# A Mamba and mixture-of-experts block on one core: B and C projected as rows, read by ScalarE in slot 21

## The chip, the cores and the metric

The kernel runs on one core of one Trainium2 chip. The metric is the device time of one execution in microseconds (us); the figure for the kernel before is a median of three runs.

## What is computed

The input x has 32 sequences of 256 tokens with 128 channels. Three residual steps follow one another: half a mixture-of-experts FFN on the layernorm of x, a Mamba step on the layernorm of the result, and half the same FFN again. All is fp32.

```python
x = x + 0.5 * ffn(layernorm(x))
x = x + mamba(layernorm(x))
x = x + 0.5 * ffn(layernorm(x))
# in mamba(x):
x_in, z = split(x @ W_in + b_in)
x_conv = silu(causal_conv4(x_in))
Bm, Cm = split(x_conv @ W_xp + b_xp)          # 16 states each
delta = softplus(x_conv @ W_dt + b_dt)
h_t = exp(delta_t * A) * h_(t-1) + delta_t * x_conv_t * Bm_t
y = sum_states(h * Cm) + D_skip * x_conv
out = layernorm(x + (y * silu(z)) @ W_out + b_out, alpha, beta)
```

The FFN (`ffn`) has a router that takes the best two of 8 experts of width 176 and a shared expert of width 352; the kernel computes all experts and weights them.

## The kernel before

The 32 sequences are cut into 16 groups of two, 512 tokens each. `iterations` runs k from -2 to 17; iteration k scans group k, while the group ahead is prepared (layernorm, convolution, projections), a later one runs through the first FFN and the one behind through the second. Every iteration has 32 slots, two for each of the 16 states. What an engine does in a slot stands in tables written out by hand: `PLAN` names the steps, `UNIT` says in which slot a chunk of 128 FFN rows begins, `SP_PLAN` orders SyncE's DMAs. `PLANS` and the like hold variants for the first and the last iterations; iterations 2 to 13 use `PLAN` itself. Each engine runs its queue in order, and semaphores tie them together.

One FFN chunk that begins in slot s goes like this. TensorE makes h1 and h2 in slot s (L1173, L1197) into two alternating PSUM buffers each. ScalarE takes silu of h1 in the same slot (L796). VectorE multiplies h2 in slot s+1 (L991) by a row of router weights, `wrow`, that SyncE has brought by DMA (L507), or by silu for the shared expert. GpSimd multiplies that by silu in slot s+2 (`gated`, L649). TensorE makes the down product into `ps_y` in slot s+4 (L1189). An h1 product waits for the silu two chunks before it, and an h2 product for VectorE's product two chunks before it.

One state of the scan goes like this, in even slots. TensorE spreads one row of B over all partitions (`row_b`, L1152) into the upper half of `ps_db`, VectorE multiplies it by `du` (L966) in the odd slot before, ScalarE has made the decays (L779), VectorE scans (`hist`, L1011), and GpSimd multiplies by the row of C (`prod`, L718), which came by DMA (`crow`). After every second product GpSimd issues a DMA that adds the pair into `yacc` (L735).

B is wanted as three bf16 parts that add up to the fp32 value, stacked on 96 partitions (`bT`), so that `row_b` is a bf16 product. The kernel before makes them so: step `xproj` (L1261) multiplies each of four token tiles by the 32 columns of `w_xp`, which gives tokens on partitions; `bparts` (L1074, L1075) on VectorE adds the bias and rounds; `bsplit` (L686 to L688) on GpSimd makes the other two parts; `cT` and `bT` turn C and B by four transposes each (L1131), and ScalarE copies them out of PSUM (L845, L848). SyncE stores C to a DRAM tensor and reads rows back, spread over partitions.

All small products share one PSUM buffer, `ps_m`. Their steps take it in turns in the order of the plan: `claim` waits until the step before has been read (`misc_taken`).

SyncE loads the constants of the Mamba step in iteration -2, slot 8 (`other_constants`, L543), between the `wrow` DMAs of the first FFN. In slot 22 it stores the finished x of an old group, waits for that, and loads the next, after `addy1` in slot 21 has added the last down product into x (L998).

## Time and profile before

| | |
|---|---|
| median of 3 runs | 1823.36 us (1817.59 to 1824.13) |
| profiled execution, its own time | 1825.36 us |
| profiled execution, span from first to last instruction | 1823.6 us |
| mean granted TensorE clock | 0.973 |
| busy: TensorE, VectorE, ScalarE, GpSimd | 1653.7, 1484.8, 1270.4, 1444.2 us |
| moved by DMA | 302.97 MB |

A busy time is the sum of an engine's instructions in the one profiled execution. A time of idleness in brackets stands before the instruction that ended it, with what released it. Matmul ends are modelled, so neighbours overlap in the rows; start to start is the surer measure. An fp32 product shows as two records.

### The profile page before, as it was taken

How to read it: one execution, taken by the hardware profiler on the slowest of the kernel's cores; microseconds unless marked ns; L12 is line 12 of the kernel's file. 1: busy time of each engine (PE TensorE's matmuls, PEld its weight loads, DVE VectorE, ACT ScalarE, POOL GpSimd, SP SyncE). 2: the span in 40 equal slices, each digit the busy share in tenths (PEclk: the TensorE clock that was granted, in tenths of full speed). 3: DMA queues.
4: the chain of work that ended last, by engine and by line, in shares of the span. 5: the costliest groups of instructions: out<-in, count | busy, mean ns of one | idle time of the engine just before them, and what ended most of it. 6: DMA issues, size and time to landing. Idle time of an engine off the chain costs nothing.

```text
span 1823.6 us, 24045 instructions
## 1 busy us (share of the span) xinstructions
PE 1653.7 (91%) x7378; PEld 999.5 (55%) x7378; DVE 1484.8 (81%) x2244; ACT 1270.4 (70%) x2034; POOL 1444.2 (79%) x1362
## 2 busy tenths in 40 slices
PE   7877688999999999999999999999999999976689
PEld 4543445566565555656555555655555565543356
DVE  3276789889898988989898998979898898978852
ACT  3375678787868777786877777787777778675522
POOL 5255778888888888888888888889898888887853
PEclk9999799999999999999999999999999999998789
DMA  6136568687777868686777868777686868677632
GB/s 183 41 94 156 143 150 205 160 195 174 186 185 165 195 153 199 153 201 169 183 184 169 197 159 193 178 185 186 160 207 152 191 167 192 168 162 179 161 88 76
DMA packets 120999, 302.97 MB, mean 166 GB/s; under 512 B 19267, under 2 KB 40486, under 8 KB 106662
## 3 DMA queue, kind: packets, MB, share of 16 engines
q0 software_dynamic: 18144, 124.26, 34.1%
q1 hardware_dynamic: 100214, 175.36, 34.0%
q10 hardware_dynamic: 2512, 1.81, 0.3%
q8 instruction: 58, 0.95, 0.2%
q14 instruction: 71, 0.58, 0.1%
HBM read 167.67 MB, written 5.24 MB: 95 GB/s over the span
## 4 chain that ended last, share of the span: by engine, by line
POOL 46%; DMA 23%; issue 15%; PE 8%; DVE 5%; ACT 2%; SPq 0%; POOLq 0%; DVEq 0%; ACTq 0%
DMA yacc<-prod 21%; POOL prod L718 19%; POOL gated L649 14%; POOL yacc L714 3%; PE ps_y L1189 3%; DVE hist L1011 2%; POOL yacc L735 1%; PE ps_h1a L1173 1%; DVE ps_db L966 1%; PE ps_h2b L1197 1%; PE ps_h2a L1197 1%; POOL xres L705 1%; PE ps_h1b L1173 1%; POOL rstdx L630 1%; POOL prob L672 1%
## 5 line engine op out<-in xcount | busy, mean ns | idle before, releaser
L718 POOL TENSOR_TENSOR prod<-hist,crow 128x1024 f32<-128x1024 f32 x224 | 557.2, 2487 | 224.4 <-DVE hist L1011 192.9
L1189 PEld LDWEIGHTS ps_y<-down_w,gated 128*128 128x128 f32 (+1 forms) x3584 | 476.7, 196 | 278.0 <-issue 167.4
L1011 DVE TENSOR_TENSOR_SCAN hist<-decay,ps_db 128x1024 f32<-128x1024 f32 x256 | 583.3, 2279 | 3.8 <-ACT decay L779 1.1
L649 POOL TENSOR_TENSOR gated<-gated,silu 128x512 f32<-128x512 f32 x352 | 492.8, 1446 | 71.0 <-DVE gated L991 67.7
L1189 PE MATMUL ps_y<-down_w,gated 128*128 128x128 f32 (+1 forms) x3584 | 492.0, 282 | 54.2 <-POOL gated L649 51.2
L966 DVE TENSOR_TENSOR ps_db<-du,ps_db 128x1024 f32<-128x1024 f32 x256 | 313.2, 1223 | 135.2 <-PE ps_db L1152 133.4
L779 ACT ACTIVATE decay<-delta,a_neg 128x510 f32<-128x510 f32 x512 | 326.8, 709 | 1.5
L796 ACT ACTIVATE silu<-ps_h1a 128x512 f32<-128x512 f32 (+1 forms) x224 | 132.9, 593 | 189.0 <-PE ps_h1a L1173 186.2
L1173 PE MATMUL ps_h1b<-xnT,up_w 128*128 128x512 f32 x448 | 234.5, 605 | 8.1 <-ACT silu L796 8.1
L1173 PE MATMUL ps_h1a<-xnT,up_w 128*128 128x512 f32 (+1 forms) x448 | 238.4, 614 | 1.4 <-ACT xnT L802 1.0
L1197 PE MATMUL ps_h2b<-xnT,up_w 128*128 128x512 f32 x448 | 236.4, 610 | 0.6 <-DVE gated L991 0.5
L1197 PE MATMUL ps_h2a<-xnT,up_w 128*128 128x512 f32 (+1 forms) x448 | 233.1, 602 | 3.7 <-DVE gated L991 3.7
L796 ACT ACTIVATE silu<-ps_h1b 128x512 f32<-128x512 f32 x224 | 133.0, 594 | 77.5 <-PE ps_h1b L1173 70.5
L991 DVE TENSOR_TENSOR gated<-ps_h2b,wrow 128x512 f32<-128x512 f32 x192 | 130.7, 681 | 68.0 <-DMA wrow<-w_rows 36.1
L779 ACT ACT_TABLE_LOAD x126 | 161.7, 1283 | 2.2
L796 ACT ACT_TABLE_LOAD x113 | 145.0, 1283 | 2.0
L1152 PE MATMUL ps_db<-bT,sel_b 96*128 96x512 bf16 x256 | 101.7, 397 | 40.2 <-DVE hist L1011 39.8
L991 DVE TENSOR_TENSOR gated<-ps_h2a,wrow 128x512 f32<-128x512 f32 x160 | 107.9, 674 | 26.6 <-PE ps_h2a L1197 21.4
L1141 PE MATMUL ps_m<-xnT,w_conv 128*128 128x512 f32 (+3 forms) x256 | 119.2, 599 | 5.1 <-ACT xnT L802 5.1
L1173 PEld LDWEIGHTS ps_h1a<-xnT,up_w 128*128 128x128 f32 (+1 forms) x448 | 86.3, 195 | 57.9 <-issue 44.9
L1173 PEld LDWEIGHTS ps_h1b<-xnT,up_w 128*128 128x128 f32 x448 | 78.6, 192 | 66.3 <-issue 37.7
L735 POOL DMA_DIRECT2D yacc<-prod x111 | 100.8, 909 | 2.3 <-issue 2.3
(139 smaller groups left out, 1931.0 us busy)
## 6 DMA issues: line engine op xcount, KB each, us to landing
yacc<-prod POOLq DMA_DIRECT2D x111, 1024.0 KB, 9.9
crow<-c_rows SPq DMA_DIRECT2D x128, 512.0 KB, 5.0
wrow<-w_rows SPq DMA_DIRECT2D x320, 128.0 KB, 6.0
wrow<-w_rows SPq DMA_DIRECT2D x64, 224.0 KB, 7.3
wrow<-w_rows SPq DMA_DIRECT2D x64, 192.0 KB, 5.3
wrow<-w_rows SPq DMA_DIRECT2D x64, 160.0 KB, 3.0
yacc<-yacc POOLq DMA_DIRECT2D x15, 512.0 KB, 7.8
wrow<-w_rows SPq DMA_DIRECT2D x64, 96.0 KB, 3.0
```

The costliest lines, as they stand in the source:

```text
L649: nc.gpsimd.tensor_tensor(gated[:, pos % NGATE, :], gated[:, pos % NGATE, :], silu[:, (pos + NCHUNK * f_parity(of, f)) % NSILU, :], ALU.mu ...
L718: nc.gpsimd.tensor_tensor(prod[:, (pair - 1 + odd) % 2, s % 2, :, :], hist[:, s % 2, :, :], c_all, ALU.mult).then_inc(prod_done, 1)
L735: pool.dma_start(yacc[odd][:], prod[:, (pair - 1 + odd) % 2, :, :, :], accum_op=ALU.add).then_inc(acc_done, 16)
L779: ins = nc.scalar.activation(decay[:, s % NA, half, :, 1:LEN], d[:, :, 1:LEN], ACT.Exp, scale=a_neg[:, half, s:s + 1])
L796: nc.scalar.activation(silu[0:r, (pos + NCHUNK * f_parity(of, f)) % NSILU, :], ps_h1[pos % 2][0:r, :], ACT.Silu).then_inc(silu_done, 1)
L966: nc.vector.tensor_tensor(ps_db[:].rearrange("p (h t) -> p h t", h=HALVES), du[par][:], ps_db[:, TG:2 * TG].unsqueeze(1).to_broadcast([P, ...
L991: nc.vector.tensor_tensor(gated[0:r, pos % NGATE, :], ps_h2[pos % 2][0:r, :], factor, ALU.mult).then_inc(h2_taken, 1)
L1011: nc.vector.tensor_tensor_scan(hist[:, s % 2, :, :].rearrange("p h t -> p (h t)"), decay[:, s % NA, :, :, :].rearrange("p h b t -> p (h b ...
L1141: nc.tensor.matmul(acc[:, :, late:LEN], w_conv[:, tap, half * P:(half + 1) * P], now[:, :, 0:LEN - late], start=(tap == PAD), stop=False)
L1173: nc.tensor.matmul(ps_h1[pos % 2][0:r, :], up_w[:, 0, j * P:j * P + r], xnT[f][:], start=True, stop=True).then_inc(h1_full, 1)
L1189: ins = nc.tensor.matmul(ps_y[:, t * C:(t + 1) * C], gated[0:rd, posd % NGATE, t * P:(t + 1) * P], down_w[0:rd, jd, :], start=(posd == 0 a ...
L1197: nc.tensor.matmul(ps_h2[pos % 2][0:r, :], up_w[:, 1, j * P:j * P + r], xnT[f][:], start=True, stop=True).then_inc(h2_full, 1)
```

## The change

The projection gives rows at once. The weights `w_rows_bc` have 112 columns: the 16 of B at 0, 32 and 64, the 16 of C at 96, and zeros between. Two fp32 products of 512 tokens (one for each half of the 256 inputs) leave B three times and C once in `ps_m`, states on partitions. ScalarE reads the 96 rows of B with their bias, rounded to bf16, into `bT` (`b_high`), and then the 16 rows of C with their bias into `bounce`. VectorE takes bias + product - rounded value on the first 64 rows (`b_rest`), which frees `ps_m`. ScalarE rounds that into the first 64 rows of `bT` (`b_mid`), and GpSimd subtracts the middle part on the first 16 (`b_low`). So `bT` holds the low, the middle and the high part on its three blocks. `bparts`, `bsplit`, `cT` and `bT` are gone as steps; `bounce` has rows of its own for C. The constants come by eight DMAs in place of two, after VectorE has zeroed the padding.

```diff
@@ -56,8 +57,8 @@
         6: ["norm2", "rcopy0"], 7: ["gate_y0", "xT2"], 8: ["gate_y1", "in0a"], 9: ["in0"], 10: ["outproj"],
         11: ["resid", "route0"], 12: ["stats3", "in1a", "tilt0"], 13: ["in1", "scale3"], 14: ["in2", "ln_norm", "weights0"],
         15: ["in3", "ln_scale"], 16: ["wT0", "ln_shift"], 17: ["dt0"], 18: ["dt1", "ln_add"], 19: ["stats1"],
-        20: ["sp_exp", "xproj", "scale1"], 21: ["addy1"], 22: ["norm1", "sp_ln", "bparts"], 23: ["xT1", "bsplit"], 24: ["logits1"],
-        25: ["rcopy1", "route1"], 26: ["cT", "delta"], 27: ["bT", "tilt1"], 28: ["weights1", "du"], 30: ["wT1"],
+        20: ["sp_exp", "xproj", "scale1"], 21: ["addy1", "b_high"], 22: ["norm1", "sp_ln", "b_rest"], 23: ["xT1", "b_mid"], 24: ["logits1"],
+        25: ["rcopy1", "route1"], 26: ["delta"], 27: ["b_low", "tilt1"], 28: ["weights1", "du"], 30: ["wT1"],
     }
     EARLY = ("addy0", "addy1", "resid")
...
@@ -108,7 +109,7 @@
         24: ["store_w0@1", "w0:0@1", "w0:1@1", "w0:2@1", "w0:3@1"],
     }
     PLANS[-1] = {
-        0: ["sp_exp", "xproj"], 1: ["sp_ln", "bparts"], 2: ["bsplit", "a_neg"], 3: ["delta", "cT"], 4: ["bT"],
+        0: ["sp_exp", "xproj", "b_high"], 1: ["sp_ln", "b_rest"], 2: ["b_mid", "a_neg"], 3: ["delta"], 4: ["b_low"],
         5: ["du", "in2"], 6: ["in3"], 7: ["bias_parts"],
     }
     UNITS[-1] = {2: (0, 6), 4: (0, 7)}
@@ -116,8 +117,8 @@
     PLANS[0] = {
         1: ["stats0"], 2: ["scale0"], 3: ["norm0"], 6: ["xT0"], 7: ["logits0"], 8: ["rcopy0", "route0"], 9: ["addy0", "tilt0"],
         10: ["weights0", "stats2"], 11: ["scale2", "wT0"], 12: ["norm2"], 14: ["xT2"], 15: ["in0a"], 16: ["in0"],
-        17: ["in1a"], 18: ["in1"], 19: ["dt0"], 20: ["dt1"], 22: ["sp_exp", "xproj"], 23: ["sp_ln"], 24: ["bparts"],
-        25: ["bsplit", "in2"], 26: ["delta", "cT"], 27: ["bT"], 28: ["du", "in3"],
+        17: ["in1a"], 18: ["in1"], 19: ["dt0"], 20: ["dt1"], 22: ["sp_exp", "xproj", "b_high"], 23: ["sp_ln"], 24: ["b_rest"],
+        25: ["b_mid", "in2"], 26: ["delta"], 27: ["b_low"], 28: ["du", "in3"],
     }
     UNITS[0] = {pos - 8: (0, pos, -1) for pos in range(8, NCHUNK)}
...
@@ -367,12 +363,10 @@
         dtmp = sb("dtmp", [P, HALVES, TG])
         delta = [sb(f"delta{i}", [P, HALVES, TG]) for i in range(2)]
         du = [sb(f"du{i}", [P, HALVES, TG]) for i in range(2)]
-        bc = sb("bc", [P, TILES, 2 * NS])
-        brem = sb("brem", [P, TILES, NS])
-        bparts = sb("bparts", [P, TILES, KP], BF16)
+        brem = sb("brem", [64, TG])
         bT = [sb(f"bT{i}", [KP, TG], BF16) for i in range(2)]
-        bounce = sb("bounce", [NS, TG])
-        wT, cT = bounce[0:E, :], bounce
+        bounce = sb("bounce", [BC_ROWS, TG])
+        wT, cT = bounce[0:E, :], bounce[KP:BC_ROWS, :]
         NA, NC = 4, 4
         decay = sb("decay", [P, NA, HALVES, NSEQ, LEN])
...
@@ -477,7 +472,7 @@
             def rows_c(g, par, p):
 
                 if p == 0:
-                    sp.wait_ge(misc_taken, turn(g - 1, "cT"))
+                    sp.wait_ge(c_made, g + 1)
                     sp.dma_start(c_rows[par, :, :], cT[:]).then_inc(c_stored, 16)
                 if p > 1 or g > 0:
...
@@ -542,12 +537,20 @@
             def const(dst, src, sem):
                 sp.dma_start(dst, src).then_inc(sem, 16)
 
+            def dve_zeroed():
+
+                sp.wait_ge(pads_zero, 3)
+
             def other_constants():
                 with nc.allow_non_contiguous_dma(reason="small constants in column form"):
                     const(w_dt[:], W_dt.rearrange("(h p) n -> p h n", p=P), consts_loaded)
                     const(b_dt_c[:], b_dt.rearrange("(h p) -> p h", p=P), consts_loaded)
-                    const(w_xp[:], W_xp.rearrange("(h p) n -> p h n", p=P), consts_loaded)
-                    const(b_xp_b[:], b_xp.partition_broadcast(P), consts_loaded)
+                    dve_zeroed()
+                    for q in range(PARTS):
+                        const(w_rows_bc[:, :, 32 * q:32 * q + NS], W_xp[:, 0:NS].rearrange("(h p) n -> p h n", p=P), consts_loaded)
+                        const(b_rows_bc[32 * q:32 * q + NS, :], b_xp[0:NS].rearrange("(n o) -> n o", o=1), consts_loaded)
+                    const(w_rows_bc[:, :, KP:BC_ROWS], W_xp[:, NS:2 * NS].rearrange("(h p) n -> p h n", p=P), consts_loaded)
+                    const(b_rows_bc[KP:BC_ROWS, :], b_xp[NS:2 * NS].rearrange("(n o) -> n o", o=1), consts_loaded)
                     const(a_log[:], A_log.rearrange("(h p) s -> p h s", p=P), consts_loaded)
                     const(d_c[:], D_skip.rearrange("(h p) -> p h", p=P), consts_loaded)
...
@@ -679,14 +682,10 @@
                             nc.gpsimd.tensor_tensor(wtok[:], hotp[:, :, 0, :], hotp[:, :, 1, :], ALU.add
                                                     ).then_inc(wtok_ready, 1)
                             chain.end()
-                        elif step == "bsplit":
-                            pool.wait_ge(misc_taken, turn(it, "xproj"))
-                            chain = Chain(pool, pool_split, SPLIT_LINKS, it + 1)
-                            hi, md, lo = (bparts[:, :, 32 * q:32 * q + NS] for q in range(PARTS))
-                            chain.link(nc.gpsimd.tensor_tensor(md, bc[:, :, 0:NS], hi, ALU.subtract))
-                            chain.link(nc.gpsimd.tensor_tensor(brem[:], bc[:, :, 0:NS], hi, ALU.subtract))
-                            nc.gpsimd.tensor_tensor(lo, brem[:], md, ALU.subtract).then_inc(bparts_ready, 1)
-                            chain.end()
+                        elif step == "b_low":
+                            pool.wait_ge(b_mid_ready, it + 2)
+                            low = bT[nxt][0:NS, :]
+                            nc.gpsimd.tensor_tensor(low, brem[0:NS, :], low, ALU.subtract).then_inc(b_ready, 1)
                         elif step == "fold":
                             pool.wait_ge(acc_done, 16 * PAIRS * it)
...
@@ -836,17 +835,10 @@
                             take(it, step)
                             if route_no(it, step) > 0:
                                 act.wait_ge(w_stored, 16 * route_no(it, step))
-                            if bounced(it, step, ("cT",)) > 0:
-                                act.wait_ge(c_stored, 16 * bounced(it, step, ("cT",)))
                             nc.scalar.activation(wT, ps_m[0:E, :], ACT.Copy, scale=0.5).then_inc(misc_taken, 1)
-                        elif step == "cT":
-                            take(it, step)
-                            act.wait_ge(w_stored, 16 * bounced(it, step, ("wT0", "wT1")))
-                            nc.scalar.activation(cT[:], ps_m[0:NS, :], ACT.Copy).then_inc(misc_taken, 1)
-                        elif step == "bT":
-                            take(it, step)
-                            nc.scalar.activation(bT[nxt][:], ps_m[0:KP, 0:TG // 2].bitcast(BF16),
-                                                 ACT.Copy).then_inc(misc_taken, 1)
+                        elif step == "b_mid":
+                            act.wait_ge(misc_taken, turn(it, "xproj"))
+                            nc.scalar.activation(bT[nxt][0:64, :], brem[:], ACT.Copy).then_inc(b_mid_ready, 1)
                         elif step in ("in0", "in1"):
                             half = int(step[2])
                             if tail(it):
@@ -878,7 +870,15 @@
                     elif slot in DECAYS and scans(k):
                         decays(k, odd, DECAYS[slot])
                     for step, it in steps(k, slot):
-                        if step == "sp_exp":
+                        if step == "b_high":
+                            take(it, "xproj")
+                            nc.scalar.activation(bT[1 - it % 2][:], ps_m[0:KP, :], ACT.Identity, bias=b_rows_bc[0:KP, :]
+                                                 ).then_inc(b_high_ready, 1)
+                            if it >= 0:
+                                act.wait_ge(c_stored, 16 * (it + 1))
+                            nc.scalar.activation(cT, ps_m[KP:BC_ROWS, :], ACT.Identity, bias=b_rows_bc[KP:BC_ROWS, :]
+                                                 ).then_inc(c_made, 1)
+                        elif step == "sp_exp":
 
                             act.wait_ge(softplus_chain, (HALVES + 1) * (it + 2) - 1)
...
@@ -1065,15 +1066,15 @@
                             dve.wait_ge(delta_ready, it + 2)
                             nc.vector.tensor_tensor(du[nxt][:], delta[nxt][:], xconv[nxt][:], ALU.mult
                                                     ).then_inc(du_ready, 1)
-                        elif step == "bparts":
+                        elif step == "b_rest":
                             dve.wait_ge(misc_full, turn(it, "xproj"))
                             if it == -1:
                                 dve.wait_ge(consts_loaded, 16 * N_CONSTS)
-                            rows_in = ps_m[:, 0:TILES * 2 * NS].rearrange("p (t n) -> p t n", t=TILES)
-                            bias = b_xp_b[:].unsqueeze(1).to_broadcast([P, TILES, 2 * NS])
-                            nc.vector.tensor_tensor(bc[:], rows_in, bias, ALU.add)
-                            nc.vector.tensor_tensor(bparts[:, :, 0:NS], rows_in[:, :, 0:NS], bias[:, :, 0:NS], ALU.add
-                                                    ).then_inc(misc_taken, 1)
+                            dve.wait_ge(b_high_ready, it + 2)
+                            dve.wait_ge(c_made, it + 2)
+                            nc.vector.scalar_tensor_tensor(brem[:], ps_m[0:64, :], b_rows_bc[0:64, :],
+                                                           bT[nxt][0:64, :], ALU.add, ALU.subtract
+                                                           ).then_inc(misc_taken, 1)
                         elif step == "sum":
                             dve.wait_ge(acc_done, 16 * (PAIRS * it - 1))
...
@@ -1216,14 +1217,6 @@
                             pe.wait_ge(wtok_ready, route_no(it, step) + 1)
                             claim(it, step)
                             to_rows(wtok, E, ident, ps_m).then_inc(misc_full, 1)
-                        elif step == "cT":
-
-                            pe.wait_ge(bparts_ready, it + 2)
-                            claim(it, step)
-                            to_rows(bc[:, :, NS:2 * NS], NS, ident, ps_m).then_inc(misc_full, 1)
-                        elif step == "bT":
-                            claim(it, step)
-                            to_rows(bparts, KP, ident_bf, ps_m[:, 0:TG // 2].bitcast(BF16)).then_inc(misc_full, 1)
                         elif step == "edge":
                             pe.wait_ge(taps_made, 6)
                             claim(it, step)
@@ -1256,11 +1249,9 @@
                         elif step == "xproj":
                             pe.wait_ge(misc_taken, turn(it, "in1"))
                             claim(it, step)
-                            for t in range(TILES):
-                                for half in range(HALVES):
-                                    ins = nc.tensor.matmul(ps_m[:, t * 2 * NS:(t + 1) * 2 * NS],
-                                                           xconv[nxt][:, half, t * P:(t + 1) * P], w_xp[:, half, :],
-                                                           start=(half == 0), stop=(half == HALVES - 1))
+                            for half in range(HALVES):
+                                ins = nc.tensor.matmul(ps_m[0:BC_ROWS, :], w_rows_bc[:, half, :], xconv[nxt][:, half, :],
+                                                       start=(half == 0), stop=(half == HALVES - 1))
                             ins.then_inc(misc_full, 1)
                         elif step == "outproj":
                             pe.wait_ge(yg_ready, it)
@@ -1278,7 +1269,7 @@
                                                            stop=(t == TILES - 1 and half == HALVES - 1))
                             ins.then_inc(misc_full, 1)
                     if slot == SLOTS - 1 and lead(k):
-                        pe.wait_ge(misc_taken, turn(k, "bT"))
+                        pe.wait_ge(b_ready, k + 2)
                         if k == -1:
                             pe.wait_ge(consts_made, MADE_FIRST + MADE_REST)
                         row_b(k + 1, 1 - odd, 0)
```

In the plan of the steady iterations, GpSimd's instructions move in two places. The first piece is before, the second after, from the `gated` of slot 23 to the router weights of slot 28; `bparts`/`brem` are the split, `bT<-brem,bT` is `b_low`, `gated` the FFN, `prod` the products 12 and 13, `prob`, `hotp`, `wtok` the router weights.

```order
L649 TENSOR_TENSOR gated<-gated,silu 128x512
L686 TENSOR_TENSOR bparts<-bc,bparts 128x4x16
L687 TENSOR_TENSOR brem<-bc,bparts 128x64
L688 TENSOR_TENSOR bparts<-brem,bparts 128x4x16
L649 TENSOR_TENSOR gated<-gated,silu 128x512
L718 TENSOR_TENSOR prod<-hist,crow 128x1024
L649 TENSOR_TENSOR gated<-gated,silu 128x512 x2
L718 TENSOR_TENSOR prod<-hist,crow 128x1024
L727 TENSOR_TENSOR carrier_p<-pow_half,pow_mone 128x1
L735 DMA yacc<-prod 128x2048
L649 TENSOR_TENSOR gated<-gated,silu 128x512 x2
L672 TENSOR_TENSOR prob<-tilt,pow_mone 128x8
```

```order
L652 TENSOR_TENSOR gated<-gated,silu 128x512 x2
L717 TENSOR_TENSOR prod<-hist,crow 128x1024
L652 TENSOR_TENSOR gated<-gated,silu 128x512 x2
L717 TENSOR_TENSOR prod<-hist,crow 128x1024
L726 TENSOR_TENSOR carrier_p<-pow_half,pow_mone 128x1
L734 DMA yacc<-prod 128x2048
L652 TENSOR_TENSOR gated<-gated,silu 128x512
L688 TENSOR_TENSOR bT<-brem,bT 16x512
L652 TENSOR_TENSOR gated<-gated,silu 128x512
L675 TENSOR_TENSOR prob<-tilt,pow_mone 128x8
L678 TENSOR_TENSOR hotp<-hot,prob 128x64
L682 TENSOR_TENSOR wtok<-hotp 128x32
```

The three instructions of slot 23 have left, and one on 16 partitions stands in slot 27 between the two `gated` of slots 27 and 28, ahead of the router weights.

On ScalarE, in the same iterations, from the silu of slot 21 to that of slot 24 (`xn` and `xnT` are the second FFN's input and its transpose, `dtmp` the softplus); first before, then after.

```order
L796 ACTIVATE silu<-ps_h1b 128x512
L796 ACTIVATE silu<-ps_h1a 128x512
L766 ACTIVATE xn<-xres,nbias,rstd 128x128 x4
L873 ACT_TABLE_LOAD
L873 ACTIVATE dtmp<-dtmp 128x1024
L796 ACT_TABLE_LOAD
L796 ACTIVATE silu<-ps_h1b 128x512
L802 ACTIVATE xnT<-ps_m 128x512
L796 ACTIVATE silu<-ps_h1a 128x512
```

```order
L795 ACTIVATE silu<-ps_h1b 128x512
L875 ACTIVATE bT<-ps_m,b_rows_bc 96x512
L879 ACTIVATE bounce<-ps_m,b_rows_bc 16x512
L795 ACTIVATE silu<-ps_h1a 128x512
L765 ACTIVATE xn<-xres,nbias,rstd 128x128 x4
L865 ACT_TABLE_LOAD
L865 ACTIVATE dtmp<-dtmp 128x1024
L795 ACT_TABLE_LOAD
L795 ACTIVATE silu<-ps_h1b 128x512
L801 ACTIVATE xnT<-ps_m 128x512
L841 ACTIVATE bT<-brem 64x512
L795 ACTIVATE silu<-ps_h1a 128x512
```

Two reads of `ps_m` have come in front of the silu of slot 22 and of all that follows, and one copy in front of that of slot 24. The two reads that stood in slots 26 and 27 have left.

## Rows read from the trace of the kernel before

**Rows 1.** The page: busy us, share of the span, instructions.
```profile
PE 1653.7 (91%) x7378; PEld 999.5 (55%) x7378; DVE 1484.8 (81%) x2244; ACT 1270.4 (70%) x2034; POOL 1444.2 (79%) x1362
```

**Rows 2.** Timeline of TensorE, steady groups: start, us, engine, line, op, names, [idle before].
```profile
1094.54 1.95 PE L1252 MATMUL ps_m<-xconv,w_dt 128*128 128x512 f32 x4 [1.01 <-ACT dpre L869]
1100.88 1.87 PE L1261 MATMUL ps_m<-w_xp,xconv 128*128 128x32 f32 x16
...
1114.37 1.06 PE L1212 MATMUL ps_m<-wg,xnT 128*128 128x8 f32 x8 [0.22 <-ACT xnT L802]
...
1120.81 0.60 PE L1131 MATMUL ps_m<-ident,bc 128*16 128x128 f32 x4
1123.86 0.39 PE L1131 MATMUL ps_m<-ident_bf,bparts 128*96 128x128 bf16 x4
...
1130.19 1.16 PE L1189 MATMUL ps_y<-down_w,gated 128*128 128x128 f32 x8 [1.27 <-POOL gated L649]
...
1136.79 1.16 PE L1189 MATMUL ps_y<-down_w,gated 128*128 128x128 f32 x8 [0.45 <-POOL gated L649]
...
1218.86 1.06 PE L1212 MATMUL ps_m<-wg,xnT 128*128 128x8 f32 x8 [0.22 <-ACT xnT L802]
...
1337.89 1.16 PE L1189 MATMUL ps_y<-down_w,gated 128*128 128x128 f32 x8 [1.04 <-POOL gated L649]
```

**Rows 3.** Timeline of GpSimd in the same group, slot 23 to the next slot 2.
```profile
1114.26 0.61 POOL L686 TENSOR_TENSOR bparts<-bc,bparts 128x64 bf16<-128x64 f32 x1
...
1116.82 2.37 POOL L718 TENSOR_TENSOR prod<-hist,crow 128x1024 f32<-128x1024 f32 x1
...
1124.48 3.25 POOL L718 TENSOR_TENSOR prod<-hist,crow 128x1024 f32<-128x1024 f32 x1 [2.85 <-DVE hist L1011]
...
1128.55 2.81 POOL L649 TENSOR_TENSOR gated<-gated,silu 128x512 f32<-128x512 f32 x2
...
1135.47 2.49 POOL L649 TENSOR_TENSOR gated<-gated,silu 128x512 f32<-128x512 f32 x2
...
1149.39 2.37 POOL L714 TENSOR_TENSOR yacc<-hist,crow 128x1024 f32<-128x1024 f32 x1 [0.25 <-DVE hist L1011]
```

**Rows 4.** VectorE: three rows of that group, one of k = 1, one sum.
```profile
1109.62 0.27 DVE L1074 TENSOR_TENSOR bc<-ps_m,b_xp_b 128x128 f32<-128x128 f32 x1
...
1117.45 1.82 DVE L1056 TENSOR_TENSOR hot<-lanes,topi 128x64 f32<-128x64 f32 x1
...
1121.52 0.69 DVE L991 TENSOR_TENSOR gated<-ps_h2b,wrow 128x512 f32<-128x512 f32 x1 [1.11 <-DMA wrow<-w_rows]
...
284.51 0.22 DVE L1056 TENSOR_TENSOR hot<-lanes,topi 128x64 f32<-128x64 f32 x1
...
L991 DVE TENSOR_TENSOR gated<-ps_h2b,wrow 128x512 f32<-128x512 f32 x117 | 79.6, 680 | 9.2 <-DMA wrow<-w_rows 9.2
```

**Rows 5.** Timeline of ScalarE in the same group.
```profile
1097.12 0.68 ACT L869 ACTIVATE dpre<-ps_m,b_dt_c 128x512 f32<-128x512 f32 x1
...
1113.72 0.59 ACT L802 ACTIVATE xnT<-ps_m 128x512 f32<-128x512 f32 x1
```

**Rows 6.** Timeline of TensorE, slots 29 and 31 of group k = 7.
```profile
921.15 1.71 PE L1189 MATMUL ps_y<-down_w,gated 128*128 128x128 f32 x8 [1.90 <-POOL gated L649]
...
928.80 1.05 PE L1189 MATMUL ps_y<-down_w,gated 128*128 128x128 f32 x8
```

**Rows 7.** Timeline of TensorE, k = 0, slot 26.
```profile
194.34 0.85 PE L1131 MATMUL ps_m<-ident,bc 128*16 128x128 f32 x4 [4.35 <-ACT zs L860]
```

**Rows 8.** Timelines of SyncE, VectorE and TensorE in iteration -2.
```profile
26.67 0.47 SPq L543 DMA_DIRECT2D w_xp<-L_attn_W_xp  x1
...
35.49 0.69 DVE L991 TENSOR_TENSOR gated<-ps_h2b,wrow 128x512 f32<-128x512 f32 x1 [2.26 <-DMA wrow<-w_rows]
...
37.12 1.02 PE L1197 MATMUL ps_h2b<-xnT,up_w 128*128 128x512 f32 x2
```

30 lines of the change are left out of this document (15 added, 15 removed).

## Prediction

> **What bounds the kernel now.** I read the page first: TensorE is busy 91% of the span and GpSimd 79% [rows 1]. Those are averages over a ramp and a drain, so I then took the timelines of one steady group, engine by engine, and looked only at what stands in brackets: the idle time before an instruction and its releaser. The same pattern comes once a group. The router product of the second FFN opens at 1114.37 and again at 1218.86 [rows 2], a period of 104.5 us; twelve groups run in this form (k = 2 to 13).
>
> In that period TensorE waits at few places. It waits 1.01 us inside the dt products, 0.22 at the router product, 1.27 at the down product of slot 29 and 0.45 at that of slot 31 [rows 2]. The last two are released by GpSimd's `gated`. The reader should see in [rows 3] why: GpSimd waits 2.85 us for scan 13 before product 13, and from 1124.48 on no row shows an idle time until 0.25 us before 1149.39. So from slot 26 to the next group's slot 2 GpSimd is the bound, TensorE follows it at slots 29 and 31, and after that TensorE works nearly without a gap until the next group's slot 26. What holds scan 13 is on VectorE: it waits 1.11 us for the weight row `wrow` in slot 26 [rows 4]. Between 400 and 1424 us, ten groups, these products waited 9.2 us for `wrow` in all [rows 4], 0.9 a group; by the timelines nine of the twelve steady groups have the wait and three have none. That weight row is issued behind store and load of x, which follow the `addy1` of slot 21, so its landing follows TensorE's slot 21 and nothing that this change moves.
>
> **The change, part by part.** Times against the profiled execution: span 1823.6, its own time 1825.36, which is 2.0 above the median of 1823.36; I add the sum to the median.
>
> *TensorE.* Out go the 16 records of the old projection (1.87), the four transposes of C (0.60) and the four of B (0.39) [rows 2]. In come four records of 512 columns with 128-row inputs, the shape of a dt product: 1.95 [rows 2]. Net -0.91 us per group. The transposes sat in slots 26 and 27, just ahead of the 1.27 us wait of slot 29, which ends when GpSimd is done. So in the steady groups this gain only lengthens that wait: 0.
>
> *ScalarE.* In slot 21, behind the silu, come two Identity reads with a bias; that form takes 0.68 [rows 5], about 0.58 start to start. In slot 23 comes the bf16 copy, for which the nearest row is the 0.59 copy [rows 5]. Bounds 0.5 to 0.69 each. So the copy `xnT` of slot 23 is 1.16 later, and silu of slots 24 and 25 are 1.7 later. TensorE's router product then waits 0.22 + 1.16 = 1.4 instead of 0.22, and its h1 product in slot 27, which wants the silu of slot 25, about 0.3. The two old reads in slots 26 and 27 go. Together TensorE is about 0.5 later when it comes to slot 29 (1.5 of waits less 0.99 of transposes), and 1.27 of slack is there; in the groups with the least it is 1.04 [rows 2]. Price 0. If that cover were gone, 0.5 per group would show.
>
> *VectorE.* The two small adds (0.27 for the first, the second shorter) become one read of 64x512 from PSUM; the nearest row is a gate product of 512 columns, 0.69 [rows 4]. Bounds 0.27 and 0.69; I take 0.69, since length goes by columns. That is +0.3 in slot 22, before a wait for TensorE. Later, `hot` took 1.82 [rows 4] and ended at 1119.2, just when product 12 (1116.82 + 2.37 [rows 3]) ended; in a group where it met no product it took 0.22 [rows 4]. By the Trainium skill (SBUF — State Buffer, "Who interferes with whom") a VectorE instruction with two SBUF inputs and a GpSimd one that reads SBUF exclude each other, and the one that starts first keeps the ports for its whole length; the trace agrees with this. With the split gone product 12 starts 1.3 earlier and `hot` gets short. But VectorE spends that gain waiting, first for B's row 13 from a TensorE that is 1.16 later, then for `wrow`. So scan 13 stays. In the three groups without the `wrow` wait I add 0.25 each for the later row 13: +0.7.
>
> *GpSimd.* Out of slot 23 go three small instructions, 0.61 for the first and the others shorter [rows 3]. They stood before the 2.85 us wait: gain 0. Into slot 27, between the two `gated` of 1128.55, goes one 16x512 subtraction. No row shows GpSimd on 16 partitions. The bounds are 0.3, if time goes by the number of elements (8192, as the small split had), and 1.25, if it goes by columns (half of 2.49 for two `gated` of 512 columns [rows 3]). I take 1.25: ScalarE's rows show that its length doesn't follow partitions, and nothing suggests otherwise here. The Trainium skill (GPSIMD Engine Reference, "Instruction dispatch") says that each of the eight cores works on its own 16 partitions only; by it sixteen rows keep one core as long as 128 rows keep eight, and the sum is the same as mine; by the count of elements the sum would be some 9 us lower. Which holds no run here has shown.
>
> Behind the subtraction are queued the second `gated`, `prob` and its two followers (the one of them that meets `du` on VectorE waits for it, before and after the change alike), product 14 and the `gated` pair of 1135.47. TensorE waits for the first of that pair at 1136.79, with 0.45 already [rows 2]. So slot 31 moves by the whole 1.25, and as TensorE runs without a gap from there to the next `addy1`, the period becomes 105.7. In eight of the twelve steady groups the pattern is this one: 8 x 1.25 = +10.0.
>
> In the other four TensorE's clock drops to 1.2 GHz after the slot 29 wait: after 1.90 us of it the down product takes 1.71 where 1.16 is usual, and slot 31 comes 7.65 us later, not 6.60, with no wait [rows 6, 2]. There 1.05 of the 1.25 is covered: 4 x 0.3 (0.2, and a little for the later slots) = +1.2.
>
> *Ramp and end.* In group k = 0 TensorE stands 4.35 us before the transposes of C, because `ps_m` is held until ScalarE reads z behind its exponentials [rows 7]. Without the transposes TensorE goes on to B's row 14. Bounds 0 and -4.35; ScalarE is up to 1.7 later there, and z's second product still waits for it. I take -3.5. In k = -1 and k = 1 gains and losses of about 1 us meet: 0. In k = 14 GpSimd waits for scans anyway: 0.
>
> *Constants.* SyncE issues six more small DMAs at 0.47 plus a gap of 0.04 each [rows 8], 3.1 us, ahead of the first `wrow` of the later experts. VectorE waited 2.26 for it at 35.49, done at 36.2; TensorE's next h2 product into that buffer came at 37.12 [rows 8]. Slack 0.9, so +2.0 (bounds 0 and 3.1).
>
> Sum: 10.0 + 1.2 + 0.7 - 3.5 + 2.0 = +10.4; 1823.36 + 10.4 = 1833.8, so **1834 us**.
>
> **The rivals.**
> *Absorbed.* The subtraction is short (0.3) or hides. Then 8 x 0.3 + 0 + 0.7 - 3.5 + 2.0 = +1.6: 1825. For it: 16 of 128 partitions. Against: columns set the time of every other kind of row.
> *Faster: TensorE sets the pace.* The slot 29 wait shrinks because scan 13 comes earlier: with `hot` some 1.5 shorter VectorE reaches slot 26 sooner, if `wrow` is there. Then the 0.91 saved on TensorE counts, and GpSimd's extra 1.25 starts from an earlier point. 12 x -0.9 less the 1.5 of the ramp gives about -12: 1811. It decides if the 1.11 wait for `wrow` is gone. Against it: that wait is in nine of twelve groups and nothing speeds up the load.
> *Clock and ScalarE.* The waits of TensorE now lie at four places, 1.4, 0.3, 0.8 and 1.7. If they drop the clock in all twelve groups, each pays the 1.05 of [rows 6] once: 8 x 1.05 = +8.4 on top: 1842. For it: 1.9 us did it in one group; against: about the same length left it up in others.
> *The change doesn't do what it says:* that C and B's transposes stayed. The order of instructions rules it out.
>
> **How the numbers follow.** A measurement of this kernel tells 0.5% (9.1 us) from no change. Main case 0.55, own range 1827 to 1840, of which 0.35 is above 1832.5 and 0.20 below. Absorbed 0.19. Faster 0.13. Clock 0.13. Range: from 1820, which leaves most of the faster rival out, to 1843. Slower 0.35 + 0.13 = 0.48; same 0.20 + 0.19 = 0.39; faster 0.13.
>
> **What would show each step.** The 16x512 row on GpSimd near 1.25 us; TensorE's wait at slot 31 grown from 0.45 to 1.7 and at slot 29 shrunk below 1.27; router wait near 1.4; `hot` down to some tenths; period near 105.7; the 4.35 wait gone; TensorE waiting some 2 us near 37 us. The forecast is wrong if the subtraction takes 0.3, if scan 13 moves, or if slot 31's wait stays at 0.45.

## The result, and the profile after the change

| | before | after |
|---|---|---|
| median of the runs | 1821.03 us (4 runs) | 1854.97 us (4 runs, 1852.0 to 1858.4) |
| ratio | | 1.0171, 95% interval 1.0139 to 1.0203 |
| span of the profiled execution | 1823.6 us | 1853.9 us |

The kernel got 1.7% slower, clear of noise. The direction was forecast, the size was not: +33.9 us by the medians and +30.3 us of span in the two profiles, against +10.4. The page after, for [rows 1]:

```profile
PE 1661.4 (90%) x7058; PEld 982.7 (53%) x7058; DVE 1491.6 (80%) x2229; ACT 1283.7 (69%) x2050; POOL 1444.4 (78%) x1330
```

No engine's share tells the story: TensorE ran 320 records fewer and was busy 8 us longer. So I followed one instruction that stands in both programs once or twice a group, the router product, and noted how much later it starts after the change. The difference of two neighbouring entries is what the stretch between them cost; a k in brackets is the iteration of that stretch.

| router product at (before) | later by | added in the stretch | my term |
|---|---|---|---|
| 49.76 (k = -2) | 4.74 | +4.7 | constants +2.0 |
| 126.03 (k = -1) | 7.32 | +2.6 | 0 |
| 224.06 (k = 0) | 3.22 | -4.1 | -3.5 |
| 319.04 (k = 1) | 6.49 | +3.3 | 0 |
| 381.98 to 1532.58 (11 periods) | 8.07 to 22.89 | +14.8 | with the rows on either side: |
| 381.98, 1628.86 (either side of them) | 8.07, 26.37 | +1.6, +3.5 | +11.9 |
| 1722.76 (k = 14, 15) | 30.43 | +4.1 | 0 |

The steady groups cost 19.9 us where I had 11.9. Ramp and end cost 10.6 where I had -1.5: most of the miss, 12 of 20 us, lies there.

Now the steady group that answers to [rows 2]. Timeline of TensorE after the change:

```profile
1117.45 1.88 PE L1253 MATMUL ps_m<-xconv,w_rows_bc 128*112 128x512 f32 x4
...
1127.73 0.66 PE L1132 MATMUL ps_m<-ident,xn 128*128 128x128 f32 x4 [0.35 <-ACT xn L765]
...
1132.50 1.06 PE L1213 MATMUL ps_m<-wg,xnT 128*128 128x8 f32 x8 [1.28 <-ACT xnT L801]
...
1139.26 1.13 PE L1174 MATMUL ps_h1b<-xnT,up_w 128*128 128x512 f32 x2 [0.16 <-ACT silu L795]
...
1146.34 1.16 PE L1190 MATMUL ps_y<-down_w,gated 128*128 128x128 f32 x8 [0.51 <-POOL gated L652]
...
1153.73 1.16 PE L1190 MATMUL ps_y<-down_w,gated 128*128 128x128 f32 x8 [1.24 <-POOL gated L652]
```

The reader should see six things, five of them forecast: the projection takes 1.88, the router wait went from 0.22 to 1.28, slot 27's h1 product waits 0.16, slot 29's wait shrank from 1.27 to 0.51 and slot 31's grew from 0.45 to 1.24. The sixth is the wait of 0.35 that the transposes of `xn` (step `xT1`) now have. Timeline of GpSimd in the same group, for [rows 3]:

```profile
1140.62 3.25 POOL L717 TENSOR_TENSOR prod<-hist,crow 128x1024 f32<-128x1024 f32 x1 [3.04 <-DVE hist L1012]
...
1145.92 1.15 POOL L688 TENSOR_TENSOR bT<-brem,bT 16x512 bf16<-16x512 f32 x1
1147.04 1.26 POOL L652 TENSOR_TENSOR gated<-gated,silu 128x512 f32<-128x512 f32 x1
1148.27 1.17 POOL L675 TENSOR_TENSOR prob<-tilt,pow_mone 128x8 f32<-128x8 f32 x1
...
1150.10 2.35 POOL L717 TENSOR_TENSOR prod<-hist,crow 128x1024 f32<-128x1024 f32 x1
```

The subtraction on 16 partitions takes 1.15 us, against 1.26 for a `gated` on 128, both of 512 columns. So time goes by columns here. (The Trainium skill, GPSIMD Engine Reference, "Instruction dispatch", gives each core its own 16 partitions; this row agrees with it.) Timelines of VectorE and then ScalarE, for [rows 4, 5]:

```profile
1134.97 0.23 DVE L1057 TENSOR_TENSOR hot<-lanes,topi 128x64 f32<-128x64 f32 x1
1136.52 1.23 DVE L967 TENSOR_TENSOR ps_db<-du,ps_db 128x1024 f32<-128x1024 f32 x1 [1.32 <-PE ps_db L1153]
1137.66 0.68 DVE L992 TENSOR_TENSOR gated<-ps_h2b,wrow 128x512 f32<-128x512 f32 x1
```

```profile
1124.70 0.68 ACT L879 ACTIVATE bounce<-ps_m,b_rows_bc 16x512 f32<-16x512 f32 x1
1125.40 0.60 ACT L795 ACTIVATE silu<-ps_h1a 128x512 f32<-128x512 f32 x1
```

Slot 26's `gated` no longer waits for `wrow` in this group, nor in ten more of the twelve (one still waits, 0.17); VectorE waits for row 13 of B from TensorE instead.

What my sum lacked in the steady groups is in the windows from router product to router product. TensorE, columns: window, length, busy (records), granted clock, DMA share, GB/s. Before the change:

```profile
1010.50:1114.37 103.87, 99.94 (x462) 1.00 0.76 181
1114.37:1218.86 104.49, 100.38 (x462) 1.00 0.77 180
...
1426.54:1532.58 106.04, 101.70 (x461) 0.98 0.75 179
```

After:

```profile
921.15:1025.99 104.84, 99.70 (x441) 1.00 0.75 180
1025.99:1132.50 106.51, 101.09 (x442) 0.98 0.75 176
1132.50:1237.36 104.86, 99.71 (x442) 1.00 0.74 179
```

After the change a period has one of two lengths, by whether the clock fell to its half level (1.2 GHz) in it: 4 of 11 at full clock, 104.97 on average, and 7 with a stretch at half clock, 106.51. All seven stretches begin right behind the router product's 1.28 us wait (granted clock 0.50 from 1028 to 1030). Before, 7 periods are at full clock, 104.15 on average, and 4 have a stretch behind slot 29's wait [rows 6], 105.39; but there the two kinds overlap (103.25 to 105.21 and 105.06 to 106.04), since the lateness of the weight row sets the length too.

A steady period comes apart at GpSimd's product 13, and the two parts have causes of their own. The first runs from the start of the projection (1100.88 before, 1117.45 after) to product 13, the second from there to the next projection. Means of 11 periods, experiments included:

| profile | projection to product 13 | product 13 to the next projection |
|---|---|---|
| before, 7 at full clock | 23.27 (22.37 to 24.32) | 80.88 |
| before, 4 with half clock behind slot 29 | 23.81 | 81.59 |
| after, 4 at full clock | 23.29 | 81.68 |
| after, 7 with half clock behind the router product | 24.81 | 81.70 |
| experiment 2 (subtraction in slot 26) | 24.40 | 80.86 |
| experiment 5 (only the reads, half clock in all) | 24.88 | 80.88 |
| experiment 6 (only the subtraction) | 23.30 | 81.55 |

The second part holds the subtraction: +0.81, or 8.9 us in 11 periods, less 2.8 for the four half-clock stretches of before, which are gone. The first part holds ScalarE's reads. Row 13 of B started on TensorE 17.09 behind the projection before, 18.66 after at full clock, and 20.32 with half clock. At full clock that was covered, 23.29 against 23.46 for all periods before; the half clock pushed it past the cover: +8.8 us in 11 periods, all from the seven. Together 14.9, against the 14.8 measured. A group with half clock, TensorE, VectorE and GpSimd after the change:

```profile
1025.99 1.06 PE L1213 MATMUL ps_m<-wg,xnT 128*128 128x8 f32 x8 [1.28 <-ACT xnT L801]
1026.91 1.78 PE L1174 MATMUL ps_h1b<-xnT,up_w 128*128 128x512 f32 x2
```

```profile
1031.68 1.23 DVE L967 TENSOR_TENSOR ps_db<-du,ps_db 128x1024 f32<-128x1024 f32 x1 [2.99 <-PE ps_db L1153]
```

```profile
1035.78 3.26 POOL L717 TENSOR_TENSOR prod<-hist,crow 128x1024 f32<-128x1024 f32 x1 [4.71 <-DVE hist L1012]
```

Why the clock fell in seven periods and not in the other four, with the same wait to 0.01 us, no run shows.

### The profile page after: what moved, and what is told of

It is laid out like the page before. It is cut to its first block, busy times and chain, and to the rows that moved or that the text cites. A ratio compares the mean times of both kernels' runs of the same rounds, so it can differ in the third digit from the quotient of the medians.

```text
span 1853.9 us, 23364 instructions
## 1 busy us (share of the span) xinstructions
PE 1661.4 (90%) x7058; PEld 982.7 (53%) x7058; DVE 1491.6 (80%) x2229; ACT 1283.7 (69%) x2050; POOL 1444.4 (78%) x1330
## 4 chain that ended last, share of the span: by engine, by line
POOL 43%; DMA 17%; issue 16%; PE 13%; ACT 5%; DVE 4%; SPq 1%; POOLq 0%; DVEq 0%; ACTq 0%
POOL prod L717 18%; DMA yacc<-prod 16%; POOL gated L652 14%; PE ps_y L1190 4%; POOL yacc L713 3%; DVE hist L1012 2%; PE ps_h1a L1174 2%; PE ps_h2b L1198 2%; PE ps_h1b L1174 1%; PE ps_h2a L1198 1%; PE ps_m L1142 1%; DVE ps_db L967 1%; ACT decay L778 1%; POOL xres L704 1%; POOL rstdx L633 1%
## 5 line engine op out<-in xcount | busy, mean ns | idle before, releaser
L1190 PEld LDWEIGHTS ps_y<-down_w,gated 128*128 128x128 f32 (+1 forms) x3584 | 484.3, 199 | 287.8 <-issue 176.0
L1190 PE MATMUL ps_y<-down_w,gated 128*128 128x128 f32 (+1 forms) x3584 | 499.7, 285 | 56.4 <-POOL gated L652 53.6
L1174 PE MATMUL ps_h1b<-xnT,up_w 128*128 128x512 f32 x448 | 242.6, 624 | 7.3 <-ACT silu L795 7.3
```

The lines of the kernel that those rows point to most:

```text
L1174: nc.tensor.matmul(ps_h1[pos % 2][0:r, :], up_w[:, 0, j * P:j * P + r], xnT[f][:], start=True, stop=True).then_inc(h1_full, 1)
L1190: ins = nc.tensor.matmul(ps_y[:, t * C:(t + 1) * C], gated[0:rd, posd % NGATE, t * P:(t + 1) * P], down_w[0:rd, jd, :], start=(posd == 0 a ...
```

## Experiments

All are timed against the kernel before on the same chip, whose median stayed between 1821.7 and 1823.0 in the four series. Single executions of one kernel lie up to 5 us either side of its median, a few as far as 9, so a difference of medians is good to a few us, and for an edit that touches one place I also read the router table of its profile. The diffs are cut to the lines that matter, and remarks behind # in them are mine. "Period" is that from 11 steady periods, as above. Theories: **GpSimd** (the prediction's: the subtraction in slot 27 sets the loss), **ScalarE and clock** (the reads delay `xnT`, TensorE waits and the clock drops), and for ramp and end, a loss at each place of its own.

### 1. The constants later

```diff
-14: ["w0:8", "w0:9", "w0:10", "load:4"],
+14: ["w0:8", "w0:9", "w0:10", "load:4", "bc_consts"],
```

The new step `bc_consts` holds the eight loads of `w_rows_bc` and `b_rows_bc`, which leave `consts` of slot 8.

> The changed kernel, with only the eight loads of the B and C weights and biases issued later: after the last row loads of slot 14 of k = -2 instead of ahead of the second load of x. Theory 'issue order' (mine): SyncE's first weight rows of the later experts issue at about 30.8 us instead of 34.7, TensorE's wait of 2.9 us at 40.1 goes and with it the half clock behind it; the router product of about 54.5 us stands at 49.8 or a little earlier, and the whole ends 4.7 us earlier than the changed kernel: about 1850. Rival 'absorbed': the 4.7 us are taken back by a wait later in the ramp (TensorE waits for GpSimd and ScalarE near 100 and 160 us anyway), and the time stays at 1855.

Measured: 1845.09 us, ratio 1.0151 (1.0116 to 1.0187): 9.9 us less than the changed kernel, twice what I expected. TensorE waits for nothing in 25 to 42 us, and the router product that stood 4.74 late at 49.76 is 0.40 late. At 126.03 it is 1.02 late, not 7.3, and at 224.06 it is 1.9 early. So the constants cost all of the first 4.7 and most of what I had counted against k = -1. Of the variants with the change's own constants and ramp, one had that 224.06 product 2.7 us late, three had it 6.2, 7.1 and 6.4 us late: this ramp costs 3 to 7 us, not 3.

### 2. The subtraction in slot 26

```diff
-26: ["delta"], 27: ["b_low", "tilt1"],
+26: ["b_low", "delta"], 27: ["tilt1"],
```

The plan of k = 0 gets the same.

> The changed kernel with GpSimd's 16x512 subtraction moved from slot 27 (between two gated products) to slot 26, ahead of product 13, where GpSimd waits about 3 us for scan 13. Theory 'GpSimd' (the one of the prediction): the 1.15 us go from a place where GpSimd is the bound to one where it waits, so each of twelve steady groups gets 0.8 to 1.15 us shorter: 10 to 14 us, about 1843. Rival 'ScalarE and clock': the subtraction is not what sets the period, the router product's wait of 1.28 us and the half clock behind it stay, the 106.5 us periods stay 106.5 in seven or eight groups, and the time falls by less than 4 us.

Measured: 1846.35 us, ratio 1.0153 (1.0119 to 1.0188): 8.6 us less. The intervals of the two kernels overlap, so the profile has to decide: the mean period fell from 105.95 to 105.26, all of it in the second part (81.69 to 80.86), but the router wait is still 1.28 and 7 of 11 periods still have half clock. The subtraction is real and worth some 8 to 9 us; it is not the whole.

### 3. C read by VectorE

```diff
 # ScalarE, step b_high, slot 21
-nc.scalar.activation(cT, ps_m[KP:BC_ROWS, :], ACT.Identity, bias=b_rows_bc[KP:BC_ROWS, :])
 # VectorE, step b_rest, slot 22, ahead of the read of the rest
+nc.vector.tensor_scalar(cT, ps_m[KP:BC_ROWS, :], b_rows_bc[KP:BC_ROWS, :], None, ALU.add)
```

> The changed kernel with the read of C's 16 rows moved from ScalarE (slot 21, 0.68 us) to VectorE (slot 22, ahead of the read of the rest). The router product's wait should shrink from 1.28 to about 0.6 in every steady group, whichever theory holds. Theory 'ScalarE and clock': the half clock behind that wait (eight groups, some 1.65 us each) goes in most of them, and row 13 of B comes 0.7 earlier: the time falls by 5 to 12 us, to about 1846. Theory 'GpSimd': GpSimd sets the period in slots 26 to 31, and an earlier TensorE only waits longer there: less than 3 us. A third way: VectorE becomes the late one, since it now has 0.7 more in slot 22: slower by up to 5.

Measured: 1839.5 us, ratio 1.0106 (1.0079 to 1.0133): 15 us less, from 0.7 us moved. The router product opens without a wait (0.62 of it moved ahead: `xT1` now waits for VectorE's read), and half clock is in 3 periods, not 7. The first part of the period is back at 23.48, and the weight row holds scan 13 again in eight of the twelve groups. This speaks for ScalarE and clock. (The profile's own time is 1847.45, 8 above the median.)

### 4. Who is first in the DMA queues

```diff
 def accumulate(k, odd, pair):
+    if k == G - 2 and pair == PAIRS:
+        place, value = w_turn(k + 1, 1, 0)
+        pool.wait_ge(w_ready[place], value)
```

> The changed kernel with one more wait on GpSimd, once in the whole program: in group k = 14 the last accumulation of products (1 MB) is issued only after the first weight row of the next FFN has landed. In the changed kernel SyncE issues that row 0.6 us behind the accumulation and it lands 9.5 us after its issue; in the kernel before it was 0.46 us ahead of it and landed in about 4. Theory 'who is first in the DMA queues': TensorE's wait of 9.1 us near 1692 falls to some 3 to 4 us and the whole gets 5 us shorter, about 1850. Rival: the row is late for another reason (its own issue time, 1 us each for eight of them), and the time stays at 1855.

Measured: 1852.94 us, ratio 1.0182 (1.0153 to 1.0212). Against the change's 1854.97 that is nothing the runs can tell; in its profile the ramp was 3.9 us longer than the changed kernel's. The place itself is clear in the profiles. Timeline of TensorE after the change, and in this variant:

```profile
1692.13 0.61 PE L1153 MATMUL ps_db<-bT,sel_b 96*128 96x512 bf16 x1 [9.06 <-DVE hist L1012]
```

```profile
1689.16 0.61 PE L1156 MATMUL ps_db<-bT,sel_b 96*128 96x512 bf16 x1 [3.09 <-DVE hist L1015]
```

The stretch that cost +4.1 cost -0.2 here. Behind it stand SyncE's and GpSimd's issues after the change:

```profile
1678.38 7.88 SPq L502 DMA_DIRECT2D wrow<-w_rows  x8
```

```profile
1677.79 0.88 POOL L734 DMA_DIRECT2D yacc<-prod  x1
```

The accumulation of 1 MB is issued 0.59 us ahead of the first weight row, and VectorE gets that row at 1687.93. I read the same two issues in all profiles of the study:

| profile | accumulation issued behind the weight row by | weight row used after its issue |
|---|---|---|
| before, and six others | 0.46 to 1.25 us | 3.6 to 4.2 us |
| this variant, and four others with its wait | 4.25 to 4.43 | 3.8 to 4.0 |
| experiment 7 | 0.33 | 7.3 |
| experiment 2 | 0.08 | 9.2 |
| after, experiment 3, and before with its logarithm in slot 23 (experiment 10) | -0.59, -0.71, -0.78 | 9.6, 9.9, 8.1 |

In the four profiles with the longest delays the stretch from 1628.86 to 1722.76 cost 3.3 to 5.5 us. So that much at the end of k = 14 hangs on half a microsecond between two queues, and any edit can flip them, the change's or another. Only this experiment sets the order on purpose; the other rows show what goes with it.

### 5. ScalarE's part alone, in the kernel before

```diff
+if step == "addy1" and it == k and 2 <= k < G - 2:      # ScalarE, slot 21, behind the silu
+    nc.scalar.activation(junk_a[0:KP, :], w_in[0:KP, 0:TG], ACT.Identity, bias=b_in_c[0:KP, 0:1])
+    nc.scalar.activation(junk_a[KP:KP + NS, :], w_in[KP:KP + NS, 0:TG], ACT.Identity, bias=b_in_c[KP:KP + NS, 0:1])
```

> The kernel before, with two more instructions on ScalarE: in slot 21 of the twelve steady groups, behind the silu, two Identity reads with a bias (96x512 and 16x512) of constants into a tile that nobody reads. C and B keep their old way, reads in slots 26 and 27 and all. Theory 'ScalarE and clock': the router product's wait grows from 0.22 to about 1.3 to 1.6 us, the clock is at half behind it in half of the groups or more, and the time rises by 6 to 14 us, to about 1832. By the prediction's term (cover of the slot 29 wait, 1.0 to 1.27 us, against some 1.1 to 1.4) it costs 0 to 4 us: at most 1826.

Measured: 1836.61 us, ratio 1.0076 (1.0053 to 1.01): +13.7 over the 1822.96 of its series, where I had priced the delay at 0. Nothing else differs from [rows 2 to 4]; the reads are of SBUF and take 0.71 and 0.72, against 0.68 each in the changed kernel. The same group, TensorE, VectorE and GpSimd:

```profile
1122.39 1.06 PE L1217 MATMUL ps_m<-wg,xnT 128*128 128x8 f32 x8 [1.28 <-ACT xnT L803]
...
1124.25 1.83 PE L1194 MATMUL ps_y<-down_w,gated 128*128 128x128 f32 x8
1125.87 1.91 PE L1202 MATMUL ps_h2b<-xnT,up_w 128*128 128x512 f32 x2
...
1137.88 1.16 PE L1194 MATMUL ps_y<-down_w,gated 128*128 128x128 f32 x8 [0.26 <-POOL gated L650]
```

```profile
1128.08 1.23 DVE L971 TENSOR_TENSOR ps_db<-du,ps_db 128x1024 f32<-128x1024 f32 x1 [2.42 <-PE ps_db L1157]
```

```profile
1132.17 3.25 POOL L719 TENSOR_TENSOR prod<-hist,crow 128x1024 f32<-128x1024 f32 x1 [4.14 <-DVE hist L1016]
```

The products behind the wait take 1.83 and 1.91 instead of 1.05 and 1.02: half clock. Row 13 of B reaches VectorE 2.47 later against the start of the group, the weight row's wait of 1.11 takes up its part, and the rest goes through: GpSimd waits 4.14 for scan 13 instead of 2.85 (+1.29), and TensorE's slot 29 wait shrinks by 1.01, but its end comes 1.27 later. That wait was no cover for this delay. All 11 periods had half clock (mean 105.76, against 104.60), so this run doesn't tell the price of the wait from that of the clock; experiment 8 does.

### 6. GpSimd's part alone, in the kernel before

```diff
+elif step == "bT" and 2 <= k < G - 2:       # GpSimd, slot 27, between the two gated products
+    nc.gpsimd.tensor_tensor(junk_p[:], w_in[0:NS, 0:TG], w_in[0:NS, 0:TG], ALU.subtract)
```

> The kernel before, with one more instruction on GpSimd: in slot 27 of the twelve steady groups (k = 2 to 13), between the two gated products, a 16x512 subtraction of constants into a tile that nobody reads. Nothing else is changed. Theory 'GpSimd' as the prediction had it: 0.8 to 1.15 us a group, 10 to 13 us in all, about 1833. If it costs 0.68 a group, as moving the real one away gave back in the run with the subtraction in slot 26, it is 8 us: about 1830. Rival: in the kernel before the weight row holds scan 13 and TensorE waits in slots 29 and 31 anyway, so the half clock behind them comes in more groups: 15 us or more.

Measured: 1829.64 us, ratio 1.0034 (1.0018 to 1.0051): +6.7, a half of the 1.25 a group that I priced. Timeline of GpSimd before, and in this variant:

```profile
1131.01 1.49 POOL L672 TENSOR_TENSOR prob<-tilt,pow_mone 128x8 f32<-128x8 f32 x1
...
1133.16 2.35 POOL L718 TENSOR_TENSOR prod<-hist,crow 128x1024 f32<-128x1024 f32 x1
```

```profile
1126.26 3.25 POOL L721 TENSOR_TENSOR prod<-hist,crow 128x1024 f32<-128x1024 f32 x1 [1.62 <-DVE hist L1014]
...
1131.56 1.03 POOL L692 TENSOR_TENSOR junk_p<-w_in 16x512 bf16<-16x512 f32 x1
...
1133.80 1.17 POOL L673 TENSOR_TENSOR prob<-tilt,pow_mone 128x8 f32<-128x8 f32 x1
...
1135.63 2.36 POOL L721 TENSOR_TENSOR prod<-hist,crow 128x1024 f32<-128x1024 f32 x1
```

From product 13 to product 14 it is 9.37 us, against 8.68 before (1124.48 to 1133.16): +0.69 for an instruction of 1.03. In the changed kernel it is 9.48: +0.80 for 1.15. The records of neighbours overlap, so a length overstates: the subtraction ends 0.68 (0.79 in the changed kernel) behind the end of the `gated` ahead of it. `prob` gave nothing back, though its record is shorter (1.49 before, 1.17 here): it ends 1.14 to 1.15 behind the end of the last `gated` in all three. (By the Trainium skill, SBUF — State Buffer, "Who interferes with whom", it and VectorE's `du` exclude each other. The rows agree: `prob` ends 0.04 to 0.06 behind the end of `du` in all three.) In the three periods with half clock behind slot 29 the second part is 81.60, against 81.59 before: there the subtraction is covered whole.

### 7. The reads of k = -1 behind the logarithm

```diff
-0: ["sp_exp", "xproj", "b_high"], 1: ["sp_ln", "b_rest"], 2: ["b_mid", "a_neg"], 3: ["delta"], 4: ["b_low"],
+0: ["sp_exp", "xproj"], 1: ["sp_ln", "b_high"], 2: ["b_rest", "a_neg"], 3: ["b_mid", "delta"], 4: ["b_low"],
```

> The changed kernel with the three reads of group k = -1 one slot later: the two of ScalarE behind the logarithm of slot 1 instead of ahead of the silu and the logarithm, the others behind them. Theory: the 2.6 us that the ramp loses between the router products of 54 and 133 us (GpSimd's gated waits for a silu that comes 1.3 later, TensorE waits 3.0 us for it at 102.8 and then runs at half clock) go: the router product of 133.4 stands near 130.8 and the whole ends 2 to 3 us earlier, about 1852. Rival: row 0 of B and delta of this group come later by as much, and nothing is gained.

Measured: 1850.42 us, ratio 1.0148 (1.0124 to 1.0173). The router product that was 7.32 late is 5.89 late, but 0.7 of the difference was there at 49.76 already; the runs don't tell this from the changed kernel. Inconclusive.

### 8. The parts together

Four edits (1 to 4) together:

> The changed kernel with the four edits of the first runs together: constants later, subtraction in slot 26, C read by VectorE, last accumulation of k = 14 behind the first weight row. If their gains add (1855 less 5 to 10, 8, 9 to 15, 4), it ends at 1820 to 1828, level with the kernel before. If subtraction and C read are two ways of freeing the same wait, their gains overlap and it is 1832. If TensorE now becomes the bound in slots 26 to 31 with its 0.9 us less work a group, it goes below the kernel before: 1812.

Measured: 1828.84 us, ratio 1.0030 (1.0015 to 1.0046): 26 us less than the changed kernel, where the four edits alone add up to 36 by their medians. They overlap; which ones do is not shown. Both additions of 5 and 6 at once in the kernel before (the larger read on 64 partitions there):

> The kernel before with both additions of the earlier runs at once, in the twelve steady groups: two Identity reads on ScalarE in slot 21 and a 16x512 subtraction on GpSimd in slot 27. Alone they cost 13.8 and 6.2 us. If the two add, 20 us: about 1843. If they hide each other (a later TensorE and a later GpSimd wait for one another), 14: about 1837. If the later TensorE takes away the cover that the subtraction had, more than 20: 1845 and above.

Measured: 1841.19 us, ratio 1.0102 (1.0085 to 1.0119): +19.5, and alone they made 13.7 and 6.7. They add. The mean period, 105.97, is the changed kernel's 105.95.

This run also parts wait and clock. The router wait is 1.27 to 1.28 in every group, but 5 of 11 periods kept full clock. In three of these the weight row was not waited for, and product 13 came 23.35 behind the projection, against 22.4 in such groups of experiment 6; in the other two it came where the late weight row put it (24.03 and 24.31). With half clock it came at 25.02 in all six. So the wait alone cost at most 1.0 of a period and nothing where the weight row was late, and the clock put 0.7 to 1.7 on top.

### 9. ScalarE's order, with the change's work untouched

```diff
-22: ["norm1", "sp_ln", "b_rest"], 23: ["xT1", "b_mid"],
+22: ["norm1", "b_rest"], 23: ["xT1", "sp_ln", "b_mid"],
```

> The changed kernel with one step moved: ScalarE's logarithm (1.06 us with two table loads, 3.6 in all) from slot 22, ahead of the copy xnT that the router product waits for, to slot 23, behind that copy. All of the change's instructions stay where they are. Theory 'ScalarE on the path of row 13': the router product's wait of 1.28 us goes in the steady groups, with it the half clock behind it, and row 13 of B, scan 13 and product 13 come earlier by as much: 8 to 13 us less, 1842 to 1847. Theory 'GpSimd sets the period': less than 3 us. If the silu of slot 24 becomes late instead (TensorE's h1 product of slot 26 waits for it), the gain is halved.

Measured: 1837.32 us, ratio 1.0073 (1.0051 to 1.0094): 17.7 us less than the changed kernel, more than I expected. The two reads, the subtraction and all else stand where the change put them. The router product opens without a wait; TensorE now waits 2.1 us for a silu in slot 26 instead, and 5 periods have half clock:

```profile
1227.70 0.95 PE L1213 MATMUL ps_m<-wg,xnT 128*128 128x8 f32 x8
...
1236.29 1.12 PE L1174 MATMUL ps_h1b<-xnT,up_w 128*128 128x512 f32 x2 [2.09 <-ACT silu L795]
```

So the reads cost what they did because they push a 3.6 us logarithm with its table loads, and `xnT` behind it, past the moment at which TensorE wants it. Either a shorter read (experiment 3) or another order takes the router's wait away.

### 10. Can it beat the kernel before?

Edits 1, 2, 4, 7 and 9 together:

> The changed kernel with five edits: constants later, reads of k = -1 behind the logarithm, subtraction in slot 26, logarithm of slot 22 behind the copy xnT, last accumulation of k = 14 behind the first weight row. C stays with ScalarE, so VectorE gets nothing. Theory: every loss of the change is met at its place, and TensorE's work is 0.9 us a group less than in the kernel before: 1812 to 1820, below the kernel before (1823). If another wait takes over (the weight row of slot 26 or 28, as in the run with C on VectorE), it ends level with it.

Measured: 1822.23 us, ratio 1.0003 (0.9991 to 1.0014). The kernel before with edit 9 alone:

> The kernel before with the same move of the logarithm to slot 23, and nothing else. Its router product waits 0.22 us, and the weight row holds scan 13: theory: at most 0.2 us a group, so no change within 3 us. It tells whether a version with that move that beats the kernel before owes it to the new projection or to the move.

Measured: 1820.0 us, ratio 0.9991 (0.998 to 1.0001). Then with the logarithm in slot 24 instead of 23, directly ahead of the exponentials, in the repaired changed kernel, in the same with the subtraction back in slot 27, and in the kernel before:

> The five edits of the run before, but with ScalarE's logarithm in slot 24, directly ahead of the exponentials of that slot: silu, logarithm, exponentials, silu. One table load (1.28 us) a group goes as well. Theory: TensorE's 2.1 us wait for the silu near the end of slot 26 goes, and with no wait left in slots 21 to 28 the steady groups get another 0.5 to 1.5 us shorter: 1806 to 1816, below the kernel before. Rival: the weight rows (slots 26 and 28) or product 12 and 13 on GpSimd hold the rest: 1822.

> The same kernel as the one with the logarithm in slot 24, but with GpSimd's subtraction back in slot 27, where the change has it. Theory of the prediction: 1.15 us in each group in which slots 29 and 31 wait for GpSimd: 10 to 13 us more than that kernel. By the runs so far (0.5 and 0.7 a group): 6 to 8 us more. If GpSimd has slack now: within 3 us.

> The kernel before with its logarithm in slot 24 and nothing else. It has a router wait of 0.22 us and a weight row that holds scan 13, so little to gain: 0 to 4 us less than the kernel before, 1818 to 1822. If the freed 1.28 us of ScalarE and the earlier silu also shorten its slots 24 to 27: 8 us less; then what e9 gains is owed to the move and not to the new projection.

Measured: 1821.39 us (1.0001, 0.9989 to 1.0013), 1831.06 us (1.0052, 1.0038 to 1.0066) and 1822.23 us (1.001, 0.9994 to 1.0025).

| profile | at full clock | with half clock | mean of 11 |
|---|---|---|---|
| before | 7 at 104.15 | 4 at 105.39 | 104.60 |
| after | 4 at 104.97 | 7 at 106.51 | 105.95 |
| repaired, logarithm in 24 | 10 at 103.65 | 1 at 105.56 | 103.82 |
| the same, subtraction in 27 | 9 at 104.52 | 2 at 105.93 | 104.78 |
| before, logarithm in 24 | 9 at 103.95 | 2 at 105.61 | 104.25 |

Two readings. The subtraction in slot 27 costs 9.7 us by the medians and 0.87 a period at full clock, when ScalarE is out of the way. And the new projection, repaired, is worth 0.4 us a period (103.82 against 104.25), or 0.1 with the logarithm in slot 23 (103.91 against 104.00); its ramp up to 381.98 was 3.9 and 1.7 us longer in the same profiles, and in the medians nothing is left. No version beat the kernel before by more than the noise. The time of the before profile is itself 3.6 above the 1821.76 of the last series, so I don't build on differences of a few us in totals of profiles.

## Why the forecast was wrong in size

- **GpSimd, right.** 1.25 for the subtraction by the columns: 1.15. It goes straight into the period, at 0.80 to 0.87 a group, since its record overlaps the one ahead by a third of a microsecond (experiment 6). `prob` waits for `du` before and after alike, as I had said. The 11.2 us of my two GpSimd terms stand against 9.7 measured in experiment 10. The four groups in which the half clock was to cover the subtraction did not come: no period after the change has its half clock behind slot 29.
- **ScalarE, the step that failed in the steady groups.** The router wait of 1.4 came as 1.28, the 0.3 in slot 27 as 0.16. Then: "1.27 us of slack is there", and "Price 0." The slot 29 wait was no slack for this. It ends when GpSimd is done, GpSimd starts after scan 13, and scan 13 needs a row that TensorE issues behind the router product: delay TensorE there and the end of its own later wait moves too. The only cover on that way was the weight row's wait of 1.11. At full clock it was about enough (product 13 at 23.29, against 23.46). With half clock behind the router's wait it was not: row 13 started 3.2 us late in place of 1.6, and product 13 came at 24.81. Experiment 5 priced the reads with the clock they cost at +13.7 in the kernel before, experiment 9 took 17.7 back from the changed one.
- **The clock.** I left it to a rival (1842, chance 0.13), for which I asked that all twelve groups drop, at the 1.05 of a stretch behind slot 29. Seven of eleven did, behind the router product, at 1.54 each. The rival had the right place; what it named, and the main sum left out, is what overran the cover. It stood on top of a sum that lacked ramp and end, and the direction of the forecast came out right through GpSimd's term alone.
- **VectorE, half right.** `hot` fell to 0.23 in nine of the twelve groups. "Scan 13 stays", because the weight row holds it: at full clock it nearly stayed, though TensorE held it and no longer the weight row; with half clock it came 1.4 later. The +0.7 was for the three groups without the weight row's wait; after the change eleven of twelve had none.
- **Constants.** Slack of 0.9 against 3.1 us of issues: +2.0. The issues shifted by 3.8 (one of them, of `d_c`, took 1.44, not 0.47), TensorE waited 2.89 at 40.09 and ran at half clock behind it (granted 0.50 from 42 to 43): +4.7 there, and by experiment 1 most of k = -1 too.
- **k = 0, right:** -3.5 forecast, -4.1 measured (-2.3 to -4.2 in the profiles of experiments 1 to 4, 7 and 9); the 4.35 wait of [rows 7] is gone and 2.40 for z stays.
- **k = 1 and k = 14, priced at 0:** +3.3 and +4.1. In k = 1 `xT1` waits 2.62 for `xn` (1.44 for `bparts` before), and `hot`, which took 0.22 there [rows 4], now meets a product and a `gated` on GpSimd and takes 1.90; I read this in the trace only and did not test it, so what k = 1 cost stays open. k = 14 is the flip of experiment 4.

## What to carry to other kernels

A wait is slack only for work that its releaser doesn't depend on: before pricing a delay at nothing, follow the releaser back and see whether it starts from the delayed engine. And a delay that just fits under its cover may bring a slower clock with it, which doesn't fit: here the same wait cost next to nothing at full clock and 1.5 us at half. New work on an engine goes behind what others wait for; here 1.4 us of reads cost little once the 3.6 us step behind them no longer stood ahead of the awaited copy. The few us won by a leaner stage are lost to an added constant load or to two DMA issues that change places, so ramp and end have to be read as closely as the steady loop.

## What was not expected of the hardware

- A wait of 1.28 us before the router product was followed by half clock in 7 of 11 periods of the changed kernel, in all 11 of experiment 5 and in 6 of 11 with both additions; the wait was the same to 0.01 us. In the changed kernel a period with a half-clock stretch took 1.54 us longer, with both additions 1.33 (106.57 against 105.24).
- Where a 1 MB accumulation was issued up to 0.8 us ahead of a weight row, or 0.08 behind it, the row was used 4 to 6 us later than where it was issued 0.46 us or more behind. At 0.33 behind, it was 3 to 4.
- ScalarE's read of 16 partitions by 512 costs what one of 96 does: 0.68 us each, 0.70 from start to start.
